# Dividing a head's projected result by its sums: eight ScalarE copies in place of one VectorE product

## The reference

```python
q, k = _apply_rope(q, cos, sin), _apply_rope(k, cos, sin)
att = jnp.einsum('bqhd,bkhd->bhqk', q, k) / jnp.sqrt(jnp.asarray(E, x.dtype))
att = jnp.where(causal, att, jnp.asarray(-jnp.inf, x.dtype))
att = jax.nn.softmax(att, axis=-1)
y = jnp.einsum('bhqk,bkhd->bqhd', att, v).reshape(B, S, H * E)
return jnp.einsum('bsf,ef->bse', y, w_o)
```

## Time and profile before

| | |
|---|---|
| median of 3 runs | 4188.31 us |
| the profiled execution's own time | 4186.24 us |
| its span | 4184.4 us |
| granted TensorE clock, mean over the span | 0.87 |
| attention loop, first to last reciprocal | 1125.8 to 3380.6 us |
| busy: TensorE matmul | 3259.0 us (78%) |
| busy: VectorE | 2927.1 us (70%) |
| busy: ScalarE | 1962.3 us (47%) |
| busy: POOL | 1730.2 us (41%) |

### The profile page before, as it was taken

One profiled execution on the slowest core, in us unless ns is written; L12 is line 12 of the kernel. 1 busy time (PEld: TensorE's weight loads), 2 busy tenths in 40 slices (PEclk: granted clock), 3 DMA queues, 4 the chain that ended last, 5 costly groups with the idle time before them and its releaser, 6 DMA issues. The chain is left out here.

```text
span 4184.4 us, 65991 instructions
## 1 busy us (share of the span) xinstructions
PE 3259.0 (78%) x19917; PEld 2498.4 (60%) x19917; DVE 2927.1 (70%) x3868; ACT 1962.3 (47%) x2883; POOL 1730.2 (41%) x1316
## 2 busy tenths in 40 slices
PE   6333333333699999999999999999999929999998
PEld 1122222222466666676667676766676729898988
DVE  2344444444688888888888888888888864565656
ACT  0001000100366666666666666666666624454545
POOL 0577777776344444444444444444444430000000
PEclk8555555555799999999999999999999969999999
DMA  3533333332444544545545444444454443333433
GB/s 88 146 95 95 95 92 94 96 94 84 130 118 121 126 121 121 126 121 126 121 120 124 112 120 120 120 119 120 115 125 115 120 94 126 107 138 107 139 107 106
DMA packets 277334, 476.75 MB, mean 114 GB/s; under 512 B 83336, under 2 KB 101528, under 8 KB 277016
## 3 DMA queue, kind: packets, MB, share of 16 engines
q1 hardware_dynamic: 249624, 400.31, 36.7%
q0 software_dynamic: 27648, 75.53, 6.1%
HBM read 246.28 MB, written 24.38 MB: 65 GB/s over the span
## 5 line engine op out<-in xcount | busy, mean ns | idle before, releaser
L1103 DVE TENSOR_TENSOR attention_probs_l<-attention_probs,attention_probs_h 128x896 fp32r<-128x896 f32 (+4 forms) x768 | 936.2, 1225 | 94.6 <-ACT attention_probs_h L1020 93.6
L1016 ACT ACTIVATE attention_probs<-attention_pss 128x896 f32<-128x896 f32 (+4 forms) x768 | 624.7, 813 | 670.2 <-PE attention_pss L878 644.8
L415 POOL DMA_INDIRECT deform_gat<-table,deform_idx x576 | 671.3, 1165 | 208.0 <-issue 156.1
L1020 ACT ACTIVATE attention_probs_h<-attention_pss 128x896 fp32r<-128x896 f32 (+4 forms) x768 | 618.1, 805 | 0.0
L1115 POOL TENSOR_TENSOR attention_qk<-attention_tA,attention_tB 128x512 f32<-128x512 f32 x260 | 430.8, 1667 | 373.1 <-DVE attention_tB L1084 341.8
L1535 DVE SCALAR_TENSOR_TENSOR spectral_eo<-spectral_psE,spectral_sig,spectral_eo 64x512 fp32r<-64x512 f32 x512 | 383.9, 750 | 263.8 <-ACT spectral_eo L1514 259.2
L875 PE MATMUL attention_pss<-attention_QA,attention_KA 128*128 128x512 f32 (+4 forms) x1536 | 502.3, 381 | 67.2 <-ACT attention_probs_h L1020 61.8
L949 PE MATMUL attention_psY<-attention_probs_h,attention_xt 128*128 128x512 f32 (+2 forms) x1548 | 509.5, 387 | 39.1 <-DVE attention_probs_l L1103 37.8
L1131 POOL TENSOR_TENSOR kept_T<-kept_T,attention_scaled 128x512 f32 x129 | 189.6, 1470 | 804.5 <-DVE attention_scaled L1058 804.5
L1069 DVE TENSOR_REDUCE attention_mx<-attention_pss 128x2 f32<-128x1024 f32 (+3 forms) x520 | 515.7, 1012 | 2.2 <-PE attention_pss L900 2.2
L1438 PE MATMUL spectral_psE<-spectral_tz,spectral_up 128*128 128x256 f32 (+2 forms) x3072 | 507.5, 324 | 4.4 <-DVE spectral_eo L1535 4.4
(11 more groups left out here) (170 smaller groups left out, 4912.0 us busy)
## 6 DMA issues: line engine op xcount, KB each, us to landing
attention_QA<-attention_nat_h SPq DMA_DIRECT2D x520, 128.0 KB, 2.4
spectral_tz<-phis SPq DMA_DIRECT2D x128, 320.5 KB, 4.5
spectral_tz<-phis SPq DMA_DIRECT2D x128, 320.0 KB, 4.2
attention_xb<-xn SPq DMA_DIRECT2D x67, 512.0 KB, 3.5
attention_wt<-wsplit SPq DMA_DIRECT2D x67, 512.0 KB, 4.2
attention_KA<-attention_nat_h SPq DMA_DIRECT2D x260, 128.0 KB, 2.4
attention_KB<-attention_nat_h SPq DMA_DIRECT2D x260, 128.0 KB, 2.4
attention_KA<-attention_nat_l SPq DMA_DIRECT2D x260, 128.0 KB, 2.4
```

The source lines that it names most:

```text
L415: pool.indirect_dma_start(gat[:, r, k, :, :].rearrange("p q c -> p (q c)"), None, d.table.rearrange("r q c -> r (q c)"), bass.IndirectOffs ...
L1016: act.activation(probs[:, j % 2, 0:width], pss[:, slot, lead:lead + width], ACT.Exp, scale=float(E) ** -0.5)
L1020: act.activation(probs_h[:, pstep[j]:pstep[j] + width], pss[:, slot, lead:lead + width], ACT.Exp, scale=float(E) ** -0.5).then_inc(s_act, 1)
L1103: dve.tensor_tensor(probs_l[:, cols], probs[:, j % 2, 0:widths(j)], probs_h[:, cols].bitcast(F32), ALU.subtract).then_inc(s_lo, 1)
```

## The change

ScalarE takes over the scaling: `scale_out` moves to it and becomes eight copies of 128x64, each with its own column of `rec` as the per-partition scale. VectorE keeps the reciprocal (`invert_sums`). `rec` gets two buffers, "out" joins `BY_ACT`, and POOL's addition waits for `s_act`. In ScalarE's program the copies stand right after the exponentials of the step in which "out" lies.

```diff
-BY_ACT = ("S", "row")
+BY_ACT = ("S", "row", "out")
...
-        rec = sb("rec", [P, NT])
+        rec = sb("rec", [P, 2, NT])
...
+                    if u[0] == "out":
+                        scale_out(slot, h % 2, BODY_HEADS * it + h)
+
+                def scale_out(slot, buffer, before):
+
+                    out = pss[:, slot, :].rearrange("p (t c) -> p t c", t=NT)
+                    wait_apart(act, s_T, before + 1, s_apart)
+                    act.wait_ge(s_rec, before + 1)
+                    for t in range(NT):
+                        ins = act.activation(scaled[:, buffer, t, :], out[:, t, 0:E], ACT.Copy, scale=rec[:, buffer, t:t + 1])
+                    ins.then_inc(s_act, 1)
...
                 leave(NIT, -1)
+                scale_out(0, 0, BODY_HEADS * NIT)
...
-                def scale_out(slot, buffer, before):
+                def invert_sums(slot, n, buffer, before):
 
                     out = pss[:, slot, :].rearrange("p (t c) -> p t c", t=NT)
-                    dve.reciprocal(rec[:, :], out[:, :, E]).then_inc(s_rec, 1)
                     wait_apart(dve, s_T, before + 1, s_apart)
-                    dve.wait_ge(s_rec, before + 1)
-                    dve.tensor_tensor(scaled[:, buffer, :, :], out[:, :, 0:E],
-                                      rec[:, :].unsqueeze(2).to_broadcast([P, NT, E]), ALU.mult).then_inc(s_dve, 1)
+                    dve.wait_ge(s_full, n + 1)
+                    dve.reciprocal(rec[:, buffer, :], out[:, :, E]).then_inc(s_rec, 1)
...
-                    wait_apart(pool, s_dve, read, s_apart)
+                    wait_apart(pool, s_act, read, s_apart)
```

More of the change, by code:

```diff
@@ L1086, in unit @@
                     if u[0] == "out":
-                        scale_out(slot, h % 2, before)
+                        invert_sums(slot, n, h % 2, before)
                 for n, (h, _, u) in enumerate(AHEAD):
@@ L1104, in _ @@
                                                   probs_h[:, cols].bitcast(F32), ALU.subtract).then_inc(s_lo, 1)
-                dve.wait_ge(s_full, N_AHEAD + N_BODY * NIT + 1)
-                scale_out(0, 0, BODY_HEADS * NIT)
+                invert_sums(0, N_AHEAD + N_BODY * NIT, 0, BODY_HEADS * NIT)
             @block.gpsimd
@@ L1151, in _ @@
                                     h = 2 * k + r
-                                    add_out(it * DVE_BODY + (DVE_AHEAD + reads_before(ORDER, outs[h], False) + 1), h % 2,
+                                    add_out(it * ACT_BODY + (ACT_AHEAD + reads_before(ORDER, outs[h], True) + 1), h % 2,
                                             b + (c + CB - 1) // CB if h == 0 else b + 1, BODY_HEADS * it + h)
-                add_out(NIT * DVE_BODY + (DVE_AHEAD + 1), 0, B, BODY_HEADS * NIT)
+                add_out(NIT * ACT_BODY + (ACT_AHEAD + 1), 0, B, BODY_HEADS * NIT)
 SEGMENTS = [(0, 64, 3), (64, 128, 2), (128, 256, 1), (256, 512, 0)]
```

## The result

The changed kernel takes 4310.68 us, the median of 4 runs (4305.27 to 4314.43), against 4187.9 us (4186.22 to 4189.85) for the kernel before: 1.0292 times as long, 95% interval 1.0274 to 1.031. That is 123 us more; 260 were forecast. The direction and the places were right, the size was forecast twice too large, and 4310.68 lies inside the stated range, near rival (c).

What follows compares the result with a forecast made beforehand. TensorE was taken to set the pace, VectorE close behind. Delays of 7.16 us per pass x 32 plus 2 us gave 231; with 29 for the clock, 260 on 4186.2: 4446, forecast as 4448 us, range 4300 to 4515.

Steps and rivals of the forecast that it cites:

- rival (c): ScalarE's eight copies per head overlap, taking 1.71 us instead of 2.46: 4322 us, up to 4351 with clock falls; chance 0.20.
- VectorE's gain is nothing: VectorE loses 129 products, 89 us, in the attention loop; at most 36 us could come back, counted as nothing.
- One copy is 0.307 us: One 128x64 copy on ScalarE from PSUM: 218 ns with fixed scale, 88 ns more for a scale per partition.
- The eight take 2.46 us, without overlap: ScalarE's eight copies per head run one after another, 8 x 0.307 = 2.46 us.
- The bound of 1.71: Lower bound for ScalarE's eight copies per head if they overlap: 0.307 + 7 x 0.20 = 1.71 us.
- The estimate from the page, 2.01 us: ScalarE's eight copies by the Trainium skill page's figures: 2.01 us, making the whole sum some 58 us lower.
- The even stop, 1.29: After an even head's "out", TensorE stops 1.29 us before `max c`, twice per pass: slot released at 2.81 us, against 1.52.
- The odd stop, 1.18: After the odd head's "out" in the middle of a pass, TensorE stops 1.18 us before S5: 2.81 - 1.63.
- S0 in the middle, 2.68: The next pair's first score in mid-pass starts 2.68 us late, waiting for `rows_b` through two DMAs; includes 1.18 of slot stop.
- the DMA path: From the end of the `rows_b` copy to the next pair's first score: taken as 2.82 us, lower bound 1.55.
- The loop's end, 1.90: A pass's first unit waits for all of ScalarE's reads; its start was forecast 1.90 us late in all.
- The clock falls once per pass, 29 us: TensorE's granted clock falls once at each pass's end, 0.9 us per fall, 29 us in total.

Runs made afterwards that it cites:

- the relief alone: Kernel before without the division: VectorE takes only the reciprocals, no 128x512 product and no copies on ScalarE; 4188.45 us, ratio 1.0001.
- the eight series: Changed kernel with series of ScalarE copies behind the last head, varying size, scale, type and partitions; 4325.0 us, one run.

## Why the prediction was wrong in its size

By its own steps:

- *VectorE's gain is nothing*: right, shown by the relief alone (1.0001).
- *One copy is 0.307 us*: right. The shortest of the 1032 took 305 ns, their median is 328.
- *The eight take 2.46 us, without overlap*: this is the step that failed. They take 1.75, a start every 0.20 us. The bound of 1.71 was close to the truth, and the choice between the bounds went by a row (L1514) that differed in what mattered: its two activations sit on different halves of the partitions. The prediction also weighed the Trainium skill, page "ScalarE: Activation LUTs", section "What ACT_TABLE_LOAD costs": activations in a row overlap by about 93 ns. Seven of the eight series agree with that (0.10 to 0.14 us), the one with alternating partitions doesn't. The prediction's words that the trace does not agree on it were wrong already by its own, where the next activation starts 0.11 us before the end of the one before. The estimate from the page, 2.01 us, was 0.26 too long.
- *The even stop, 1.29*: 0.52. With 1.71 in the same sum it is 0.54. *The odd stop, 1.18*: 0.41, by the sum 0.43. *S0 in the middle, 2.68*: 1.63, by the sum 1.93; the DMA path is 2.72 us and not 2.82, and the row copy starts 0.17 before the last of the eight ends. *The loop's end, 1.90*: 0.86, by the sum 1.15; the exponentials start 1.97 us after the reciprocal and not 2.18 (the first copy is 0.05 earlier than taken, and the row copy overlaps the last one here too), and they took 3.07 us, 2001.92 to 2004.99, and not 3.15.
- *The clock falls once per pass, 29 us*: wrong. The granted clock stays at 1.00 in 28 of 32 passes. In four it went to the lower level for 3.4 us (from 1556.6, 1857.0, 2379.2 and 3126.7), each time soon after the S0 at the loop's end, with TensorE busy 1.79 or 1.80 of the 3.5 us before. The first two rows show one fall, the third another; but as much work at 2001.90 to 2005.40, last row, left it at 1.00.

```profile
1853.40:1856.90 3.50, 1.79 (x9) 1.06 (x8) 2.05 (x2) 1.74 (x3) 0.17 (x1) 1.00 0.01 2
1856.90:1860.40 3.50, 3.50 (x10) 2.75 (x10) 1.35 (x3) 3.22 (x3) 0.26 (x1) 0.51 0.00 0
...
3126.72:3130.13 3.41, 3.41 (x10) 2.70 (x9) 1.34 (x3) 3.22 (x3) 0.25 (x1) 0.50 0.00 0
...
2001.90:2005.40 3.50, 1.79 (x9) 1.17 (x9) 1.47 (x2) 3.09 (x6) 1.30 (x1) 1.00 0.01 2
```

  A fall cost 0.6 us (0.8 the first time), not 0.9: from S0 to the next reciprocal 20.84 us (1855.62 to 1876.46) against 20.25 (2005.43 to 2025.68). The "rope" products of that pass take 3.52 us and not 2.09, but TensorE then doesn't stop for the exponentials behind the table load, as it does for 0.68 us at 2010.09, and that hides the rest. Four of them make 2.6 us.
- *Rival (c), the copies overlap, 4322 us* is what happened; it had a chance of 0.20, half of that of the forecast. The direction was no luck, since every release that the prediction called late was late; the size was wrong by the choice just named.

With the right length for the eight, the sum of the prediction is 4.16 us per pass; the pass grew by 3.53 in the places named. The first term to get right was one duration, since it stood in all four places: 0.71 us too much, 4 x 0.71 x 32 = 91 us of the 137 us error; the clock was 29 where it measured 2.6, and most of the rest is the overlap of the row copy, the DMA path and the exponentials named above.

## What to carry to other kernels

An engine's idle time is room only where nobody waits for what stands behind the new work: here ScalarE was idle for a third of the time, and four times 1.75 us of copies still cost a pass 3.5 us, because they sit on the release of a PSUM slot and ahead of a row that goes through two DMAs. Look first at the distance from the start of the buffer's last reader to the buffer's next use (1.52 us from the reciprocal here), and put what others wait for longest ahead: the same copies one place later, behind the row copy, gave back 44 of the 123 us. And before work is moved off a busy engine, take it away altogether: if the time stays (1.0001), there is nothing to win.

## What the runs showed that was not expected

Two copies in a row on ScalarE overlap by about 0.10 us, but not when they write and read different halves of the partitions: four of 682 ns took 2.77 us in turn, and four of 676 ns on the same half 2.40 us. Why is open; only copies with a scale per partition were tried on alternating halves. In the spectral stage 512 activations of L1514 alternate this way. And a wait for all readers at a loop's start cost 1.5 us per pass, nearly as much as the largest single part of the change (1.63 us).
